# Context bands loaded without their empty rows, and a later first tile of each group, in a fused convolution kernel

## The reference

```python
y = einsum('bhwc,cd->bhwd', x, Wf) + bf
q, ctx, gates = y[..., :C], y[..., C:2*C], y[..., 2*C:]
for l, k in enumerate((k0, k1, k2)):          # kernels of 3x3, 5x5, 7x7, one per channel
    ctx = gelu(dwconv_same(ctx, k))
    ctx_all = ctx_all + ctx * gates[..., l:l+1]
```

## Time and profile before

| | |
|---|---|
| median of 3 runs | 5436.56 us (5429.32 to 5450.64) |
| the profiled execution | 5432.24 us, span 5430.4 us |
| DVE busy | 3303.5 us, 61% |
| PE busy | 3017.6 us, 56% |
| POOL busy | 2876.9 us, 53% |
| ACT busy | 1729.1 us, 32% |
| moved by DMA | 763.09 MB |

### The profile page before, as it was taken

How to read it: one execution, slowest core, us unless ns; L and a number is a source line. 1 busy time by engine, 2 the same in 40 slices (tenths; PEclk the granted TensorE clock), 3 DMA queues, 4 the chain that set the end, 5 groups by cost and what they waited for, 6 DMA issues and landing times. The chain is left out here.

```text
span 5430.4 us, 92964 instructions
## 1 busy us (share of the span) xinstructions
PE 3017.6 (56%) x39574; PEld 2623.4 (48%) x39574; DVE 3303.5 (61%) x4063; ACT 1729.1 (32%) x3209; POOL 2876.9 (53%) x2614
## 2 busy tenths in 40 slices
PE   2873235669644466559744466569744463455333
PEld 2872135559633365449633365469633353444222
DVE  4347843575678755575678765575788655554333
ACT  1223424622234245421233245421333242232000
POOL 1000000465566665565566765674666766677776
PEclk9965655669767666669667666669766666655555
DMA  6841174569633575559633575569633564654333
GB/s 165 169 97 22 29 139 140 145 149 223 149 97 104 127 199 171 146 141 230 140 90 104 135 190 175 155 150 238 141 106 98 149 182 133 178 171 135 109 106 93
DMA packets 776762, 763.09 MB, mean 141 GB/s; under 512 B 575244, under 2 KB 652460, under 8 KB 771916
## 3 DMA queue, kind: packets, MB, share of 16 engines
q1 hardware_dynamic: 651931, 417.24, 33.3%
q0 software_dynamic: 124416, 339.90, 21.7%
HBM read 637.12 MB, written 136.73 MB: 143 GB/s over the span
## 5 line engine op out<-in xcount | busy, mean ns | idle before, releaser
L2129 POOL DMA_INDIRECT e_gb<-corner_table,e_idx x2592 | 2862.3, 1104 | 2534.1 <-DMA e_cws<-cw_all 1084.0
L2191 DVE TENSOR_TENSOR e_vw<-e_gb,e_pc 128x1024 f32<-128x1024 f32 x576 | 774.3, 1372 | 685.4 <-DMA e_gb<-corner_table,e_idx 663.4
L2157 PE MATMUL e_pv<-shifts,e_vw 128*128 128x128 f32 x2744 | 536.7, 365 | 464.0 <-DVE e_vw L2198 463.8
L2157 PEld LDWEIGHTS e_pv<-shifts,e_vw 128*128 128x128 f32 x2744 | 440.3, 190 | 496.9 <-DVE e_vw L2198 474.6
L488 PE MATMUL e_pw<-wk,e_vt 128*64 128x64 f32 (+1 forms) x2880 | 325.1, 285 | 348.0 <-DVE e_xr L2209 221.2
L488 PEld LDWEIGHTS e_pw<-wk,e_vt 128*64 128x64 f32 (+1 forms) x2880 | 279.7, 192 | 410.1 <-issue 248.6
L502 PE MATMUL b_p<-b_x,b_tt 100*100 100x96 f32 x4096 | 398.2, 259 | 32.7 <-DMA b_tt<-zl_copies 32.7
L2167 ACT ACTIVATE e_vt<-e_pv 128x512 f32<-128x512 f32 x288 | 184.2, 640 | 727.3 <-PE e_pw L2157 726.5
L502 PEld LDWEIGHTS b_p<-b_x,b_tt 100*100 100x100 f32 x4096 | 391.0, 176 | 35.3 <-DMA b_tt<-zl_copies 35.2
L1926 ACT ACTIVATE f_xall<-f_p 64x384 f32<-64x384 f32 (+2 forms) x320 | 301.7, 1056 | 132.6 <-PE f_p L1821 130.3
L2198 DVE TENSOR_TENSOR e_vw<-e_vw 128x1152 f32<-128x1152 f32 x233 | 335.4, 1440 | 8.0
(11 more groups left out here) (309 smaller groups left out, 7094.8 us busy)
## 6 DMA issues: line engine op xcount, KB each, us to landing
b_tt<-zl_copies SPq DMA_DIRECT2D x256, 234.0 KB, 9.5
b_tt<-zl_copies SPq DMA_DIRECT2D x128, 390.0 KB
e_gb<-corner_table,e_idx POOLq DMA_INDIRECT x2592
d_px<-x_halo SPq DMA_DIRECT2D x32, 1152.0 KB
corner_table<-f_xn SPq DMA_DIRECT2D x128, 288.0 KB
f_xall<-xpad SPq DMA_DIRECT2D x10, 2400.0 KB, 16.1
x_halo<-d_xo SPq DMA_DIRECT2D x128, 144.0 KB
d_wd<-wd_rows SPq DMA_DIRECT2D x8, 1890.0 KB
```

What stands on the lines that cost most here:

```text
L2129: nc.gpsimd.indirect_dma_start(self.gb[k][:, 4 * q:4 * q + 4, :].rearrange("p a c -> p (a c)"), None, T.table[m], off)\
L2157: last = nc.tensor.matmul(dst, vw[:, a, 2 * q:2 * q + nq, :].rearrange("p k c -> p (k c)"), T.ident[:, :], start=(a == 0), stop=(a == n - ...
L2191: v.tensor_tensor(dst, self.gb[k][:, 4 * k0:4 * k1, :].rearrange("p (k a) c -> p k a c", a=4), bc(w, [128, k1 - k0, 4, C], 3), ALU.mult).t ...
```

## The change

StageB.load reads only the KS0[l] rows that hold taps, from row 2*RD0[l] - KS0[l]//2 + hi on, and writes them to the same rows of tt. StageB.zeros, new, clears the rows before and behind them for both buffers with six memsets on DVE; StageA.dve calls it once a group, behind image 1's variance. Rows that only one half uses are cleared for both and then written by the loads. StageB.first waits for it on a new semaphore b_zero. Apart from that, plan() sets due to 24 units behind the clock instead of to the clock.

```diff
--- before.py
+++ after.py
@@ -670,6 +670,8 @@
             dve.wait_ge(x_in[k % 2], 80 * G + 16 + 32 * (k // 2 + 1))
             gn.dve_sums(dve, PP, self.xs[:, k % 2, :, :], self.sq[:, :, :], i)
             gn.dve_var(dve, link, self.psn, PP, i)
+        if k == 1 and p == 0:
+            self.after.zeros(dve, G)
         if 1 <= k <= NI and p:
             for g in (0, 1) if p == 1 else (2,):
                 dve.wait_ge(S.a_c_full, 12 * G + 3 * m + g + 1)
@@ -695,7 +697,7 @@
         def sb(name, shape, dt=FP32):
             return tmp.enter_context(nc.sbuf_tensor("b_" + name, shape, dt))
         self.nc, self.T, self.st = nc, T, st
-        self.S = sems(nc, ctx, "b_t00 b_t01 b_t10 b_t11 b_t20 b_t21 b_gap b_zlw b_halo b_c0 b_c1 b_c2 b_g0 b_g1 b_g2 b_acc b_mean b_ctx b_gt")
+        self.S = sems(nc, ctx, "b_t00 b_t01 b_t10 b_t11 b_t20 b_t21 b_gap b_zero b_zlw b_halo b_c0 b_c1 b_c2 b_g0 b_g1 b_g2 b_acc b_mean b_ctx b_gt")
         S = self.S
         self.t_in = ((S.b_t00, S.b_t01), (S.b_t10, S.b_t11), (S.b_t20, S.b_t21))
         self.full, self.done = (S.b_c0, S.b_c1, S.b_c2), (S.b_g0, S.b_g1, S.b_g2)
@@ -711,15 +713,30 @@
 
     def load(self, sp, l, q):
         T = self.T
+        n = KS0[l] * PITCH
         for hi in range(2):
-            src = bass.AP(T.zlw.tensor, T.zlw.offset + ORG0[l] - PITCH * hi + 4 * q * W * ZL0,
-                          [[ZL0 - 1, W], [W * ZL0, 4], [1, LB[l]]])
-            dst = halves(self.tt[:, q % 2, OB[l]:OB[l] + 4 * LB[l]])[hi].rearrange("p (c t) -> p c t", c=4)
+            skip = (2 * RD0[l] - KS0[l] // 2 + hi) * PITCH
+            src = bass.AP(T.zlw.tensor, T.zlw.offset + ORG0[l] - PITCH * hi + skip + 4 * q * W * ZL0,
+                          [[ZL0 - 1, W], [W * ZL0, 4], [1, n]])
+            dst = halves(self.tt[:, q % 2, OB[l]:OB[l] + 4 * LB[l]])[hi].rearrange("p (c t) -> p c t", c=4)[:, :, skip:skip + n]
             sp.dma_start(dst, src).then_inc(self.t_in[l][q % 2], 16)
 
+    def zeros(self, dve, G):
+
+        for q in range(2):
+            for l in range(3):
+                lead = (2 * RD0[l] - KS0[l] // 2 + 1) * PITCH
+                n = ND0[l] * PITCH - lead - (KS0[l] - 1) * PITCH
+                assert n == lead
+                t = self.tt[:, q, OB[l]:OB[l] + 4 * LB[l]]
+                ap = apv(t, 0, [list(t.ap[0]), [LB[l], 4], [LB[l] - lead, 2], [1, lead]])
+                last = self.nc.vector.memset(ap, 0.0)
+        last.then_inc(self.S.b_zero, 1)
+
     def first(self, sp, G):
 
         n = 2 * (OB[2] + 4 * LB[2])
+        sp.wait_ge(self.S.b_zero, G + 1)
         sp.dma_start(self.tt[W:PITCH, :, :].rearrange("p k t -> p (k t)"), self.T.zgap[:, 0:n]).then_inc(self.S.b_gap, 16)
         sp.wait_ge(self.S.b_zlw, 64)
         for q in range(2):
@@ -2306,7 +2323,7 @@
             tables += StageF.table_of(P, k) is not None
             if StageF.placed(P, k) is not None:
                 if tiles == J * loaded:
-                    due = clock
+                    due = clock + 24.0
                 ready += 1
         if loaded < ready and (loaded < 2 or tiles >= J * (loaded - 1) + 6):
             load()
```

## The result

| | before | after |
|---|---|---|
| median | 5433.0 us (4 runs) | 5363.7 us (5350.4 to 5375.0, 4 runs) |
| the profiled execution, span | 5430.4 us | 5373.1 us |
| ratio, with 95% interval | | 0.9865 [0.9832, 0.9898] |

The change makes the kernel 1.35% faster, some 73 us by the ratio. That is inside the predicted range and on the predicted side, but the forecast was 112 us. The profiled execution of after was the slowest of its four, so the two profiles differ by 57.3 us only.

What follows compares the result with a forecast made beforehand. The stages were taken to set the pace until tile 216's gathers start at 4529 us, POOL's gathers from there to the end. Terms -42+12-82-1 = -113 us gave 5319 or 5323, taken as 5321; range 5275 to 5385.

Steps and rivals of the forecast that it cites:

- Part 1: Stage B: shorter band loads remove PE's waits for bands and the slow end of the stage; -42 us, bounds 0 and -60.
- Rival (c): Stage B: loads cost by runs and issues, so shorter loads give 7 of 42 us; 5356 us, chance 0.08.
- Part 2: Stage A: six memsets a group on DVE delay the work queued behind them; +12 us, bounds 0 and +16.
- Part 3: Stage F: placing the first tile 24 units later removes its stall behind the places; -82 us, bounds -40 and -105.
- in the new plan tile 77 stands there, its gathers issued a step earlier: 10 us for each of three groups, 30: End of stage F: tile 77 replaces tile 79, whose 10.4 us stall lay ahead of the last places; 30 us gained.
- the work is equal, and only the stall goes: Stage F: the same three tiles (72, 73, 74) stay between places and step 11; 24 us in group 1, 76 in sum.
- The last group: From tile 216 on: three more tiles behind D step 4 (35 us) against that step 36 us earlier; -1 us net.
- (b): Stage F: tile 72's gathers begin as before and the next pairs stall DVE, half of Part 3; 5362 us, chance 0.10.
- (a): Last group: D step 4 doesn't move and POOL stays 3 tiles behind, +35 us; 5356 us, chance 0.12.
- (d): Stage F: its own PE and ACT work fills the hole, so only the lag remains; slower, 5462 us, chance 0.05.
- (e): Last group and stage B: POOL doesn't wait at all and Part 1 reaches its bound; 5280 us, chance 0.05.
- The signs: Trace marks expected per stage, such as stage A 3 to 4 us longer and image 4's places some 35 us earlier.

Runs made afterwards that it cites:

- E2: Kernel before with only the first tile placed 24 units later, full band loads and no zeros; 0.9896, or 5376 us.
- E4: The whole change, but due set back by one spacing when the places of image 12 come, restoring the old plan from tile 216; 0.9864, or 5359 us.
- E7: The whole change (24 units), but zeros brought by 20 SP transfers a group from DRAM instead of memsets; 0.9856, or 5355 us.
- E6: The whole change with the first tile 36 units behind its places instead of 24; 0.9775, or 5311 us.
- E1: Kernel before with the shorter band loads and the zeros, the plan left as before; 0.9941, or 5401 us.
- E3: Kernel before with only the six memsets a group and the wait for them, full band loads, old plan; 1.0024, or 5446 us.
- E8: The whole change, but no tile placed at steps 13 to 16 of stage F, tiles 75 to 77 going behind the last places; 0.9918, or 5388 us.
- E12: The whole change with 60 units, but spacing of tiles 157 to 215 cut to 0.9 to take the lag back in group 3; 0.9784.
- E11: The whole change with 36 units instead of 24 and zeros by 20 transfers a group from DRAM instead of memsets; 0.9767.
- E10: The whole change with the first tile 60 units behind its places instead of 24; 0.9806.

## Why the prediction was right in sign and some 40 us off in size

**Part 1 (-42 forecast, -45 measured).** Right, in size and in mechanism: the DMA share fell with the bytes, PE's waits for bands went, and the end of the stage runs at a granted clock of 1.00 instead of 0.83. (The "share 1.04 to 1.13" of the prediction leaves out the window from 300 us, where it was 0.87 and where nothing changed.) Rival (c), cost by runs and issues, falls: the issues are as many as before, and the share went from 1.04 to 0.72. The rule of the Trainium skill that I had weighed (DMA: Bandwidth & Descriptors, "Anatomy of one DMA": 2.0 us fixed, then the bytes) would have taken 8% off by my estimate, if one load followed another; with many of them under way the trace has 31%. The section gives this rule for DMAs that GpSimd issues, and SP issues these loads, so it was weighed outside of what it states.

**Part 2 (+12 forecast, +13 measured [+3, +23]).** The memsets took 752, 405 and 752 ns for the two buffers, 3.8 us a group, where I had worked out 3.9. Each stage A gets 5 us longer by them when they stand alone, so more than their own time. In the whole change it is 5.0 us for all three groups together, since the later tiles shorten it (346.3 us in E2, against 352.3 before).

**Part 3 (-82 forecast, -41 to -57 measured).** This is the term that was mis-sized, and two of its steps failed. The first is "in the new plan tile 77 stands there, its gathers issued a step earlier: 10 us for each of three groups, 30". Tile 77 stalled DVE 7.73 us directly ahead of the last places. From the second to the last places groups 0 and 1 won 4.3 and 5.5 us and group 2 lost 10.3: none of the 30 came. In group 2 the plan even puts 146, 147 and 148 behind two neighbouring steps. The second is "the work is equal, and only the stall goes". Its three tiles are miscounted: by the same plan 74 stands at step 12, so the three ahead of step 11 are 71, 72 and 73, and the gathers of 71 were long in. Nor was the stall one late tile. From the start of tile 72's gathers on POOL goes at about 12 us a tile, with one pause of 2.8 us in before and none in after, and DVE is held by it at whichever tile comes next. What the delay does is to put 2, 2 and 1 tiles fewer into that stretch (7/7/7 become 5/5/6): 5 x 11.7 = 58.5 us, and 58.2 were measured. So close a fit is luck: with the same plan in those groups E2, E4 and E7 have 53.9, 60.3 and 61.4. That the first half of the stretch alone came out near my sum, 15.5, 20.0 and 23.2 us instead of 25.3 less 8 in each group, was the right number for a wrong reason.

Of these 58 us stage C and stage F's first part gave back 14.6 and 10.1 in after and 11.2 and 10.3 in E2; I had set nothing for them. The steps behind which the tiles of a stage stand change its length though their number doesn't: with ten tiles stage C of group 1 took 142.1, 144.6 and 135.4 us in before, after and E6. It repeats with the plan: over groups 1 to 3 stage C is 425 to 430 us in the three kernels with the old plan (before, E1, E3) and 436 to 440 in the five with the new one (after, E2, E4, E7, E8), and stage F's first part 396 to 401 and 409 to 412. Which wait does it was not traced.

Stage D's +16.2 us are not a finding. The other kernels, with old plan or new, lie at 1188 to 1209 us (E12, which puts more tiles there, at 1217); before's profiled execution has the least of all, and group 0's stage D, which holds no tile, is 284.2 us in it and 285 to 290 in the others. A single execution carries such differences.

**The last group (-1 forecast).** Right: -5.4 us between the profiles, and E4 shows the cancelling from the other side. The norm ahead of D step 4 starts 96.3 us behind tile 216's first gather in before (4625.3) and 49.2 us behind it in after (4526.8), so the step comes 47 us earlier, where I had 36. POOL's waits of after from 4477, where tile 216's gathers start, to the end, against the earlier trace rows:

```profile
POOL e_gb L2146 <- issue: 208.5, 643, 12.8
POOL e_gb L2146 <- DMA e_cws<-cw_all: 7.2, 1, 7.2
POOL e_gb L2146 <- DVE e_vw L2208: 5.0, 4, 3.7
```

DVE's 24.0 us have become 5.0. That start was forecast near 4417 and came at 4477.6 (4529.0 before); from there to the end it is 895.5 us after 901.4. The error of 60 us lies all ahead of it.

**The rivals.** (b), the stalls move and half of part 3 is left, gave 5362, and the median is 5363.7. Its mechanism is the one that the runs show: POOL begins tile 72 no earlier against the places than before (11.8 us behind them, before 10.4), and the next tiles stall. I had given it 0.10 and my forecast 0.60. That the number is met within 2 us is partly luck: (b) says nothing of what stages C and F give back. The sum had the counter-evidence in it: for the end of the run I used 11.7 us a tile as POOL's own pace, but not for stage F, where the earlier trace rows has six tiles in 79.8 us (second parts from 2233.79 to 2313.55). (a) needs a longer lag, (d) fell (the stretch shrank by 58 us), and (e) too.

**The signs.** Stage B's, the bytes', the memsets' and PE's came as announced. Stage A was to be 3 to 4 us longer in each of groups 1 to 3, and was 3.5 us shorter, 1.2 longer and 7.3 longer. The places of image 4 were to be 35 us earlier and were 15.8.

**The best version that ran** is E6 (0.9775), or E11 (0.9767), which isn't told apart from it: 36 units instead of 24, 49 us below the changed kernel by the ratio, 122 below the one before. The intervals of E12 (0.9784) and E10 (0.9806) overlap with theirs, so 36 units are told apart from 24, but not surely from 48 or 60.

## What to carry to other kernels

Where one engine feeds another in order, a stall belongs to a stretch and not to the item that shows it: count the items that the plan puts between two marks, multiply by the feeder's pace, and compare with the stretch. If it fits, only fewer items in the stretch shorten it, and they must go where the feeder has time left; crowding them behind the mark (E8) makes it worse.

A delay in a plan is a debt: it is free as long as the last stretch has waits to absorb it, here up to 24 units. From 36 units on the last stretch was 18 to 36 us longer than with 24, and the delay still paid because the stages ahead of it won more. Bytes that are only zeros are worth leaving out where the profile shows the DMA share at 1; look at the share per window, not at the mean of the run.

## What the runs showed of the hardware that I had not expected

With the same number of loads and of contiguous runs, the DMA share over 100 us went from 1.04 to 0.72 as the bytes of those loads went from 28.1 to 19.2 MB a group, with a smallest load of 117 KB: at this size their fixed parts weren't to be seen.

POOL's nine gathers take 11.7 us in a stretch where the DMA share is 0.35, and 12.1 and 11.8 us in two where it is 0.62 and 0.66. So in these stretches their pace hardly depended on what else the queues carried.
